# First layer of a graph network: sums and extrema in one bank and one add, two zero matmuls an entry

## The chip, the cores and the metric

One core of one Trainium2 chip. The time is device microseconds of one execution of the whole kernel, median of the runs given. In what follows PE is TensorE, PEld its weight loads, DVE VectorE, ACT ScalarE, POOL GpSimd and SP SyncE.

## What is computed

A graph of 6250 nodes with 128 features and 206250 directed edges, sorted by destination, goes through three message-passing layers (one that aggregates in four ways, a graph convolution, a graph attention) with norms between them. The change touches only the edge loop of the first layer:

```
z2 = concatenate([node_feat[src], node_feat[dst], edge_feat], axis=-1)
e = relu(z2 @ W_pre + b_pre)
s  = segment_sum(e, dst);  sq = segment_sum(e * e, dst)
mx = segment_max(e, dst);  mn = segment_min(e, dst)
deg = segment_sum(1, dst)
```

Mean, deviation, maximum and minimum of each node then go into a two-stage network. The layers after it are the same before and after the change.

## The kernel before

Edges are in chunks of 512, destinations in windows of W = 64 nodes. An entry is one chunk seen through one window; a chunk whose edges span more than 64 nodes gets more entries, and there are 404 of them. `acc` (128 x 5 x 6400, f32, in SBUF) holds per node column the sum, the sum of squares, the count, and the maximum and minimum. The loop does for each entry:

- SP (`loads`, L520 and after, and `load_dst`) fetches the source numbers (`ms`), the edge features (`ZR`, partitions 0 to 63), 64 rows of the destination table (`WB`), the destination numbers broadcast over 64 partitions (`dstb`), and the destinations of last edges (`md`). POOL (`gather`) gathers 512 source rows (`G`) in four indirect DMAs, one for 128 rows. ACT's queue loads the segment masks (`mm2`).
- DVE: `d1` makes the one-hot of destinations in partitions 64 to 127 of `ZR`; `d2` adds the product `Z` and the gathered rows into `EE`; `hot` makes the one-hot `oh` by edges (0 to 3 for the sums, 4 to 7 for the last edge of each node); `d3` runs a maximum scan and a minimum scan over the transposed edges `ET` into `ST`; `d4a` adds sums and count from PSUM (`TT`) into `acc`, `d4b` the extrema.
- ACT: `a1` relu and square, in `EE`; `half` casts half of `oh` to bf16 (`ohb`); `a2a`, `a2b` copy the transposed scans from PSUM (`BK`) to `BS`; `e1`, `e2` copy the two products out of PSUM to `SN1` and `SN2`.
- PE: `p1` is `Z` = `ZR`^T `WB`; `p2` transposes `EE` into `ET` and makes the sums, `oh`^T times `EE`, into `S1`, in two halves of 64 columns; `t1` counts (four bf16 matmuls with ones) and turns `SN1` into `TT`; `t2` turns `SN2` into `TT`; `p3a`, `p3b` transpose the maximum and minimum scan back, one after the other through the one bank `BK`; `p4` is `oh`^T times `BS` into `S2`. `warm` is a matmul of zeros, 512 columns of bf16, into the bank that is written next; it stands ahead of `p1`, of `p2` and of `p3a`.

The order on each engine is written out by hand, by `pipeline`: a list of (lag, step), and in turn i the step runs for entry i - lag. The loop is unrolled four times. In PE's list p3a, t2, t1, p1, p3b, p2, p4 the sums of entry i - 3 and `p4` of entry i - 5 are neighbours at the end of a turn. In DVE's list `d2` comes first, for entry i - 2, and waits for the sums of entry i - 4. The waits are by semaphores with counts; what a step waits for can be read at its head. All eight banks of PSUM are in use: `Z` and `ET` two each, `S1`, `S2`, `BK`, `TT`.

Of the kernel before, what the change touches and what calls it, by code (L numbers as in the profile page):

```python
# [6 lines left out]
BF16 = mybir.dt.bfloat16  # L7
# [435 lines left out]
def phase_l0(nc, d, v):  # L443
# [10 lines left out]
    with ExitStack() as ph:  # L454
# [4 lines left out]
        dstb = sbt(ph, "dstb", [128, 4, CH])  # L459
        mm2 = sbt(ph, "mm2", [128, 4, 2, CH], BF16)  # L460
        G = sbt(ph, "G", [128, 4, 4, 128])
        EE = sbt(ph, "EE", [128, 2, 2, CH])
        oh = sbt(ph, "oh", [128, 4, 8, W])
        ohb = sbt(ph, "ohb", [128, 2, 4, W], BF16)
        ST = sbt(ph, "ST", [128, 2, 2, CH])
        BS = sbt(ph, "BS", [128, 2, 2, CH])
        SN1 = sbt(ph, "SN1", [128, 128])
        zw = sbt(ph, "zw0", [128, 128], BF16)
        zm = sbt(ph, "zm0", [128, CH], BF16)
        SN2 = sbt(ph, "SN2", [128, 128])  # L470
        Z = [pst(ph, f"Z{k}", [128, CH]) for k in range(2)]
        ET = [pst(ph, f"ET{k}", [128, CH]) for k in range(2)]
        S1 = pst(ph, "S1", [128, 512])
        S2 = pst(ph, "S2", [128, 512])
        BK = pst(ph, "BK", [128, CH])
        TT = pst(ph, "TT", [128, 512])
        S1v = TT[:, 0:3 * W].rearrange("p (a n) -> p a n", a=3)
        S2v = TT[:, 4 * W:6 * W].rearrange("p (a n) -> p a n", a=2)
# [12 lines left out]
        s_a1 = sem("l_a1")  # L491
        s_p2 = sem("l_p2")
        s_p2t = sem("l_p2t")
        s_e1 = sem("l_e1")
        s_t1 = sem("l_t1")
# [5 lines left out]
        s_e2 = sem("l_e2")  # L501
        s_t2 = sem("l_t2")
        s_d4a = sem("l_d4a")
        s_d4b = sem("l_d4b")
# [8 lines left out]
        def _(e):  # L513
# [6 lines left out]
            def loads(j):  # L520
# [5 lines left out]
                gathered, done = 64 * j.uses(4, -1), j.at(-3)  # L526
# [3 lines left out]
                if not j.first(4):  # L530
                    wait_sync(e, s_p1, done, s_sync)
                e.dma_start(ZR[0:64, k, :], src[1]).then_inc(l_in[k], 16)
                e.dma_start(WB[64:128, k, :], src[2]).then_inc(l_in[k], 16)
                if not j.first(4):
                    wait_sync(e, s_zr, done, s_sync)
                e.dma_start(dstb[64:128, k, :], src[3]).then_inc(l_db[k], 16)
# [28 lines left out]
        def _(e):  # L565
            e.memset(zw[:, :], 0.0).then_inc(s_i, 1)
            e.memset(zm[:, :], 0.0).then_inc(s_i, 1)
            e.memset(ST[:, :, :, :], 0.0).then_inc(s_i, 1)
            e.wait_ge(s_i, 3)
            T = load_T(e, tb, 0)  # L570

            def d1(j):
                k = j.slot(4)
                wait(e, l_db[k], 16 * j.uses(4))
                if not j.first(4):
                    wait(e, s_p1, j.at(-3))
                e.tensor_scalar(ZR[64:128, k, :], dstb[64:128, k, :], baseF[64:128, ds(j.at(), 1)], nid[64:128, 0:1],  # L577
                                ALU.subtract, ALU.is_equal).then_inc(s_zr, 1)

            def d2(j):  # L580
                wait(e, s_p1, j.at(1))
                wait(e, l_g[j.slot(4)], 64 * j.uses(4))
                if not j.first(2):
                    wait(e, s_p2, j.at(-1))
                e.tensor_tensor(EE[:, j.slot(2), 1, :], Z[j.slot(2)][:, :],
                                G[:, j.slot(4), :, :].rearrange("p s f -> p (s f)"), ALU.add).then_inc(s_d2, 1)

            def hot(j):
                k = j.slot(4)
                wait(e, l_md[k], 16 * j.uses(4))  # L590
                if not j.first(4):
                    wait(e, s_p4, j.at(-3))
# [1660 lines left out]
```

## Time and profile before

| | us |
|---|---|
| median of 3 runs | 5772.62 |
| lowest, highest | 5770.69, 5776.23 |
| the profiled execution | 5773.65 |
| its span, first to last instruction | 5771.7 |

The profiled execution's core had a mean granted clock of 0.947. The first layer's edge loop runs from about 130 us to 2276 us of the span; the preparation of tables lies ahead of it, the other two layers behind. In the profile a group is one line of the kernel on one engine; `idle before` is the time in which the engine did nothing just before the group's instructions, with what ended it. "issue" means that nothing the profile shows ended it.

### The profile page before, as it was taken

What the parts mean: (1) busy time and instruction counts of PE and PEld (TensorE: products, weight loads), DVE (VectorE), ACT (ScalarE), POOL (GpSimd) and SP (SyncE); (2) the same over time, 40 slices, a digit from 0 to 9 for tenths busy, and PEclk for the clock granted to TensorE, in tenths of its full rate; (3) what the DMA queues carried; (4) which work ended last, traced back from release to release, by engine and by line L of the source; (5) the groups of instructions that cost most, each with busy time, mean ns of one, the idle gap of its engine ahead of it and who ended that gap; (6) DMA issues with size and microseconds to landing.
All of it is one profiled execution on the core that took longest, in us unless ns stands there. A gap on an engine that the chain in (4) does not pass through costs nothing. (4 is left out here: it accounts for less than half of the span.)

```text
span 5771.7 us, 176467 instructions
## 1 busy us (share of the span) xinstructions
PE 5106.0 (88%) x41872; PEld 4051.2 (70%) x42482; DVE 4775.1 (83%) x12693; ACT 2880.1 (50%) x6715; POOL 3884.4 (67%) x3976
## 2 busy tenths in 40 slices
PE   3999999999999997968888866999999999999993
PEld 3888888888888886447777754666666666666663
DVE  4999999999999997767777756888888888888887
ACT  1565666656665654123333334555555555555556
POOL 2777777777777774047777724777777777777772
PEclk7999999999999998969888877999999999999996
DMA  6666666666666664322222212222222222222221
GB/s 156 160 159 159 157 158 156 159 156 158 157 157 157 158 157 119 99 53 54 54 54 53 54 33 43 54 53 53 54 53 53 53 53 53 53 53 53 53 53 48
DMA packets 667245, 544.72 MB, mean 94 GB/s; under 512 B 365794, under 2 KB 544171, under 8 KB 666853
## 3 DMA queue, kind: packets, MB, share of 16 engines
q0 software_dynamic: 126336, 262.13, 19.1%
q1 hardware_dynamic: 415050, 163.69, 12.4%
q10 hardware_dynamic: 125724, 117.57, 7.8%
q14 instruction: 108, 0.88, 0.1%
q8 instruction: 27, 0.44, 0.0%
HBM read 517.22 MB, written 25.61 MB: 94 GB/s over the span
## 5 line engine op out<-in xcount | busy, mean ns | idle before, releaser
L1766 POOL DMA_INDIRECT Gt<-TAB,metat x1632 | 1597.2, 979 | 646.9 <-issue 496.4
L559 POOL DMA_INDIRECT G<-Atab,ms x1616 | 1575.6, 975 | 576.9 <-issue 460.3
L1256 POOL DMA_INDIRECT Gc<-XS,metac x672 | 645.3, 960 | 241.8 <-issue 189.0
L1806 DVE SCALAR_TENSOR_TENSOR M<-neqt,Gt 128x256 f32<-128x256 f32 x816 | 311.0, 422 | 309.0 <-DMA Gt<-TAB,metat 308.8
L663 ACT COPY BS<-BK 128x512 f32<-128x512 f32 x808 | 465.6, 576 | 198.9 <-PE BK L752 191.1
L1401 ACT COPY acc<-CP 128x300 f32<-128x300 f32 x630 | 269.5, 428 | 555.1 <-PE CP L1439 552.4
L606 DVE TENSOR_TENSOR_SCAN ST<-mm,ST,ET 128x512 f32<-128x512 bf16 x404 | 516.7, 1279 | 0.1
L608 DVE TENSOR_TENSOR_SCAN ST<-mm,ST,ET 128x512 f32<-128x512 bf16 x404 | 506.9, 1255 | 0.0
L702 PE MATMUL Z<-WB,ZR 128*128 128x128 f32 x3232 | 429.3, 276 | 66.8 <-DVE ZR L577 66.6
L752 PE MATMUL BK<-ident,ST 128*128 128x128 f32 x3232 | 485.1, 273 | 2.4 <-ACT BS L663 1.8
L1970 PE MATMUL SR<-P,Gt 128*128 128x128 f32 x3264 | 473.7, 288 | 0.0
L1970 PEld LDWEIGHTS SR<-P,Gt 128*128 128x128 f32 x3264 | 395.8, 191 | 70.2 <-issue 70.2
L720 PE MATMUL S<-EE,oh 128*64 128x128 f32 x6464 | 442.5, 279 | 0.0
L702 PEld LDWEIGHTS Z<-WB,ZR 128*128 128x128 f32 x3232 | 428.5, 193 | 12.0
L1414 PE MATMUL OT<-acc 128*128 128x180 f32 x2100 | 431.7, 332 | 0.5 <-ACT acc L1401 0.5
L1904 ACT ACTIVATE EX<-TE,nl 128x512 f32<-128x512 f32 x408 | 294.7, 722 | 270.9 <-ACT nl L1897 140.2
L639 ACT ACTIVATE EE<-EE 128x512 f32<-128x512 f32 x404 | 255.1, 631 | 346.3 <-issue 273.1
L769 PE MATMUL S<-BS,oh 128*64 128x128 f32 x6464 | 422.5, 273 | 1.4 <-issue 1.4
L752 PEld LDWEIGHTS BK<-ident,ST 128*128 128x128 f32 x3232 | 392.6, 141 | 32.7 <-issue 2.5
L1327 DVE TENSOR_SCALAR O<-iotaD,VA 128x300 bf16<-128x300 f16 x1260 | 400.3, 322 | 1.0
L720 PEld LDWEIGHTS S<-EE,oh 128*64 128x64 f32 x6464 | 345.0, 137 | 67.7 <-issue 67.7
L1439 PE MATMUL CP<-O 128*128 128x300 bf16 x1260 | 301.2, 326 | 78.3 <-DVE O L1327 74.8
(291 smaller groups left out, 11448.5 us busy)
## 6 DMA issues: line engine op xcount, KB each, us to landing
mm<-MM ACTq DMA_DIRECT2D x404, 256.0 KB
ZR<-in_eft SPq DMA_DIRECT2D x404, 128.0 KB
dstb<-DF SPq DMA_DIRECT2D x404, 128.0 KB
Gt<-TAB,metat POOLq DMA_INDIRECT x1632
G<-Atab,ms POOLq DMA_INDIRECT x1616
ad<-ADT SPq DMA_DIRECT2D x816, 0.2 KB
WB<-Btab SPq DMA_DIRECT2D x404, 32.0 KB
Gc<-XS,metac POOLq DMA_INDIRECT x672
```

What stands on the lines that cost most here:

```text
L559: e.indirect_dma_start(G[:, k, s, :], None, Atab, bass.IndirectOffsetOnAxis(ap=ms[:, k, s:s + 1], axis=0)).then_inc(l_g[k], 16)
L606: e.tensor_tensor_scan(ST[:, q, 0, :], mm2[:, k, 0, :], ET[q][:, :], ST[:, 1 - q, 0, CH - 1:CH], ALU.mult, ALU.max)
L608: e.tensor_tensor_scan(ST[:, q, 1, :], mm2[:, k, 1, :], ET[q][:, :], ST[:, 1 - q, 1, CH - 1:CH], ALU.max, ALU.min).then_inc(s_d3, 1)
L663: e.copy(BS[:, q, a, :], BK[:, :]).then_inc(s_a2[a], 1)
L702: mm = e.matmul(Z[q][:, s * 128:(s + 1) * 128], ZR[:, k, s * 128:(s + 1) * 128], WB[:, k, :], start=True, stop=True)
L720: mm = e.matmul(S1[a * 64:(a + 1) * 64, 0:128], oh[:, k, s, :], EE[:, q, a, s * 128:(s + 1) * 128], start=(s == 0), stop=(s == 3))
L752: mm = e.transpose(BK[:, s * 128:(s + 1) * 128], ST[:, q, a, s * 128:(s + 1) * 128], ident[:, :])
L769: mm = e.matmul(S2[a * 64:(a + 1) * 64, 0:128], oh[:, k, 4 + s, :], BS[:, q, a, s * 128:(s + 1) * 128], start=(s == 0), stop=(s == 3))
L1256: e.indirect_dma_start(G[:, k, s, :], None, XS, bass.IndirectOffsetOnAxis(ap=meta[:, k, s:s + 1], axis=0)).then_inc(l_g[k], 16)
L1414: mm = e.matmul(OT[k][:, 0:DB], acc[:, 0, h * 128:(h + 1) * 128], C[k][:, h, :], start=(h == 0), stop=(h == NB - 1))
L1766: e.indirect_dma_start(G[:, k, s, :], None, TAB, bass.IndirectOffsetOnAxis(ap=meta[:, k, s:s + 1], axis=0)).then_inc(l_g[k], 16)
L1970: m = e.matmul(SR[q][:, 0:2 * W], G[:, k, s, 0:128], P[:, q, s * 128:(s + 1) * 128], start=(s == 0), stop=(s == 3))
```

## The change

- `S1` and `S2` become one bank `S`, sums in columns 0 to 127, extrema in 128 to 255. `SN1`, `SN2` become `SN` (256 columns), with one copy (`sums` on ACT) instead of two.
- `t1` and `t2` become one step `across` at lag 6: counts, then both turns. One add `d4` of 5 x 64 columns at lag 7 takes the place of `d4a` and `d4b`.
- The bank that is freed goes to `BK`: one for each scan. `p3a` and `p3b` stand one after the other at the head of PE's turn, without `warm`.
- The sums are a step of their own, `sums` at lag 5 instead of 3, between `p1` and `p2`. `EE` and `ohb` get four slots for two.
- `dstb` goes: the destination numbers are loaded into partitions 64 to 127 of `ZR`, and `d1` works in place; the load now waits for `p1` instead of for the mask.
- The zero matmul's moving operand is `zw` broadcast; `zm` goes. Orders on DVE and ACT change as the lists show.

```diff
--- before.py
+++ after.py
@@ -456,26 +456,20 @@
         md = sbt(ph, "md", [128, 4, 8], I32)
         ZR = sbt(ph, "ZR", [128, 4, CH])
         WB = sbt(ph, "WB", [128, 4, 128])
-        dstb = sbt(ph, "dstb", [128, 4, CH])
         mm2 = sbt(ph, "mm2", [128, 4, 2, CH], BF16)
         G = sbt(ph, "G", [128, 4, 4, 128])
-        EE = sbt(ph, "EE", [128, 2, 2, CH])
+        EE = sbt(ph, "EE", [128, 4, 2, CH])
         oh = sbt(ph, "oh", [128, 4, 8, W])
-        ohb = sbt(ph, "ohb", [128, 2, 4, W], BF16)
+        ohb = sbt(ph, "ohb", [128, 4, 4, W], BF16)
         ST = sbt(ph, "ST", [128, 2, 2, CH])
         BS = sbt(ph, "BS", [128, 2, 2, CH])
-        SN1 = sbt(ph, "SN1", [128, 128])
+        SN = sbt(ph, "SN", [128, 256])
         zw = sbt(ph, "zw0", [128, 128], BF16)
-        zm = sbt(ph, "zm0", [128, CH], BF16)
-        SN2 = sbt(ph, "SN2", [128, 128])
         Z = [pst(ph, f"Z{k}", [128, CH]) for k in range(2)]
         ET = [pst(ph, f"ET{k}", [128, CH]) for k in range(2)]
-        S1 = pst(ph, "S1", [128, 512])
-        S2 = pst(ph, "S2", [128, 512])
-        BK = pst(ph, "BK", [128, CH])
+        S = pst(ph, "S", [128, 512])
+        BK = [pst(ph, f"BK{a}", [128, CH]) for a in range(2)]
         TT = pst(ph, "TT", [128, 512])
-        S1v = TT[:, 0:3 * W].rearrange("p (a n) -> p a n", a=3)
-        S2v = TT[:, 4 * W:6 * W].rearrange("p (a n) -> p a n", a=2)
         l_we = sem("l_we")
         l_ms = [sem(f"l_ms{k}") for k in range(4)]
         l_md = [sem(f"l_md{k}") for k in range(4)]
...
@@ -523,17 +514,15 @@
                 e0 = c * CH
                 src = (d["meta"][ds(c, 1), :, 0:4].rearrange("a p s -> (a p) s"), d["eft"][:, ds(e0, CH)],
                        Btab[ds(b, 64), :], DF[ds(e0, CH)].partition_broadcast(64))
-                gathered, done = 64 * j.uses(4, -1), j.at(-3)
+                gathered = 64 * j.uses(4, -1)
                 if not j.first(4):
                     wait_sync(e, l_g[k], gathered, s_sync)
                 e.dma_start(ms[:, k, :], src[0]).then_inc(l_ms[k], 16)
                 if not j.first(4):
-                    wait_sync(e, s_p1, done, s_sync)
+                    wait_sync(e, s_p1, j.at(-3), s_sync)
+                e.dma_start(ZR[64:128, k, :], src[3]).then_inc(l_db[k], 16)
                 e.dma_start(ZR[0:64, k, :], src[1]).then_inc(l_in[k], 16)
                 e.dma_start(WB[64:128, k, :], src[2]).then_inc(l_in[k], 16)
-                if not j.first(4):
-                    wait_sync(e, s_zr, done, s_sync)
-                e.dma_start(dstb[64:128, k, :], src[3]).then_inc(l_db[k], 16)
 
             def load_dst(j):
                 k = j.slot(4)
@@ -564,25 +553,22 @@
         @blk.vector
         def _(e):
             e.memset(zw[:, :], 0.0).then_inc(s_i, 1)
-            e.memset(zm[:, :], 0.0).then_inc(s_i, 1)
             e.memset(ST[:, :, :, :], 0.0).then_inc(s_i, 1)
-            e.wait_ge(s_i, 3)
+            e.wait_ge(s_i, 2)
             T = load_T(e, tb, 0)
 
             def d1(j):
                 k = j.slot(4)
                 wait(e, l_db[k], 16 * j.uses(4))
-                if not j.first(4):
-                    wait(e, s_p1, j.at(-3))
-                e.tensor_scalar(ZR[64:128, k, :], dstb[64:128, k, :], baseF[64:128, ds(j.at(), 1)], nid[64:128, 0:1],
+                e.tensor_scalar(ZR[64:128, k, :], ZR[64:128, k, :], baseF[64:128, ds(j.at(), 1)], nid[64:128, 0:1],
                                 ALU.subtract, ALU.is_equal).then_inc(s_zr, 1)
 
             def d2(j):
                 wait(e, s_p1, j.at(1))
                 wait(e, l_g[j.slot(4)], 64 * j.uses(4))
-                if not j.first(2):
-                    wait(e, s_p2, j.at(-1))
-                e.tensor_tensor(EE[:, j.slot(2), 1, :], Z[j.slot(2)][:, :],
+                if not j.first(4):
+                    wait(e, s_p2, j.at(-3))
+                e.tensor_tensor(EE[:, j.slot(4), 1, :], Z[j.slot(2)][:, :],
                                 G[:, j.slot(4), :, :].rearrange("p s f -> p (s f)"), ALU.add).then_inc(s_d2, 1)
 
             def hot(j):
@@ -590,6 +576,7 @@
                 wait(e, l_md[k], 16 * j.uses(4))
                 if not j.first(4):
                     wait(e, s_p4, j.at(-3))
+                    wait(e, s_a1, j.at(-3))
                 e.scalar_tensor_tensor(oh[:, k, :, :], iotaW[:, :].unsqueeze(1).to_broadcast([128, 8, W]),
                                        baseF[:, ds(j.at(), 1)],
                                        md[:, k, :].unsqueeze(2).to_broadcast([128, 8, W]),
@@ -613,38 +600,32 @@
             def base(j):
                 keep(e, regs, j, base_of(e, tb, j))
 
-            def d4(j, S, n, lo, s_in, s_out):
+            def d4(j):
                 b = kept(e, regs, j)
-                wait(e, s_in, j.at(1))
+                wait(e, s_t, j.at(1))
                 if not j.first(1):
-                    wait(e, s_out, j.at())
-                a = acc[:, lo:lo + n, ds(b, W)]
-                e.tensor_tensor(a, a, S, ALU.add).then_inc(s_out, 1)
-
-            def d4a(j):
-                d4(j, S1v, 3, 0, s_t1, s_d4a)
-
-            def d4b(j):
-                d4(j, S2v, 2, 3, s_t2, s_d4b)
-
-            pipeline(e, T, U, D, [(4, base), (2, d2), (0, d1), (2, hot), (4, d4a), (6, d4b), (4, d3)])
+                    wait(e, s_d4, j.at())
+                a = acc[:, 0:5, ds(b, W)]
+                e.tensor_tensor(a, a, TT[:, 0:5 * W].rearrange("p (a n) -> p a n", a=5), ALU.add).then_inc(s_d4, 1)
+
+            pipeline(e, T, U, D, [(4, base), (0, d1), (7, d4), (2, d2), (2, hot), (4, d3)])
 
         @blk.scalar
         def _(e):
             T = load_T(e, tb, 0)
 
             def a1(j):
-                q = j.slot(2)
+                q = j.slot(4)
                 wait(e, s_d2, j.at(1))
                 e.activation(EE[:, q, 0, :], EE[:, q, 1, :], ACT.Relu).then_inc(s_r, 1)
                 wait(e, s_r, j.at(1))
                 e.activation(EE[:, q, 1, :], EE[:, q, 0, :], ACT.Square).then_inc(s_sq, 1)
 
             def half(j):
-                q = j.slot(2)
+                q = j.slot(4)
                 wait(e, s_oh, j.at(1))
-                if not j.first(2):
-                    wait(e, s_t1, j.at(-1))
+                if not j.first(4):
+                    wait(e, s_t, j.at(-3))
                 e.copy(ohb[:, q, :, :], oh[:, j.slot(4), 0:4, :]).then_inc(s_a1, 1)
 
             def masks(j):
@@ -660,7 +641,7 @@
                 wait(e, s_p3[a], j.at(1))
                 if not j.first(2):
                     wait(e, s_p4, j.at(-1))
-                e.copy(BS[:, q, a, :], BK[:, :]).then_inc(s_a2[a], 1)
+                e.copy(BS[:, q, a, :], BK[a][:, :]).then_inc(s_a2[a], 1)
 
             def a2a(j):
                 back(j, 0)
@@ -668,28 +649,22 @@
             def a2b(j):
                 back(j, 1)
 
-            def e1(j):
-                wait(e, s_p2, j.at(1))
-                if not j.first(1):
-                    wait(e, s_t1, j.at())
-                e.copy(SN1[:, :], S1[:, 0:128]).then_inc(s_e1, 1)
-
-            def e2(j):
+            def sums(j):
                 wait(e, s_p4, j.at(1))
                 if not j.first(1):
-                    wait(e, s_t2, j.at())
-                e.copy(SN2[:, :], S2[:, 0:128]).then_inc(s_e2, 1)
-
-            pipeline(e, T, U, D, [(5, a2a), (1, masks), (2, a1), (5, a2b), (2, half), (3, e1), (5, e2)])
+                    wait(e, s_t, j.at())
+                e.copy(SN[:, :], S[:, 0:256]).then_inc(s_e, 1)
+
+            pipeline(e, T, U, D, [(5, a2a), (5, a2b), (2, a1), (1, masks), (3, half), (5, sums)])
 
         @blk.tensor
         def _(e):
             e.wait_ge(l_we, 64)
-            e.wait_ge(s_i, 3)
+            e.wait_ge(s_i, 2)
             T = load_T(e, tb, 0)
 
             def warm(bank):
-                e.matmul(bank[:, :], zw[:, :], zm[:, :], start=True, stop=True)
+                e.matmul(bank[:, :], zw[:, :], zw[:, :].unsqueeze(1).to_broadcast([128, 4, 128]), start=True, stop=True)
 
             def p1(j):
                 q, k = j.slot(2), j.slot(4)
@@ -704,52 +679,32 @@
                 mm.then_inc(s_p1, 1)
 
             def p2(j):
-                q, k = j.slot(2), j.slot(4)
+                q = j.slot(2)
                 wait(e, s_sq, j.at(1))
                 if not j.first(2):
                     wait(e, s_d3, j.at(-1))
                 warm(ET[q])
                 for s in range(4):
-                    mm = e.transpose(ET[q][:, s * 128:(s + 1) * 128], EE[:, q, 0, s * 128:(s + 1) * 128], ident[:, :])
+                    mm = e.transpose(ET[q][:, s * 128:(s + 1) * 128], EE[:, j.slot(4), 0, s * 128:(s + 1) * 128], ident[:, :])
                 mm.then_inc(s_p2t, 1)
-                wait(e, s_oh, j.at(1))
+
+            def across(j):
+                wait(e, s_a1, j.at(1))
+                wait(e, s_e, j.at(1))
                 if not j.first(1):
-                    wait(e, s_e1, j.at())
+                    wait(e, s_d4, j.at())
                 for s in range(4):
-                    for a in range(2):
-                        mm = e.matmul(S1[a * 64:(a + 1) * 64, 0:128], oh[:, k, s, :], EE[:, q, a, s * 128:(s + 1) * 128],
-                                      start=(s == 0), stop=(s == 3))
-                mm.then_inc(s_p2, 1)
-
-            def t1(j):
-                q = j.slot(2)
-                wait(e, s_a1, j.at(1))
-                wait(e, s_e1, j.at(1))
-                wait(e, s_d4b, j.at(-2))
-                if not j.first(1):
-                    wait(e, s_d4a, j.at())
-                for s in range(4):
-                    e.matmul(TT[:, 2 * W:3 * W], onesb[:, :], ohb[:, q, s, :], start=(s == 0), stop=(s == 3))
-                e.transpose(TT[:, 0:128], SN1[:, :], ident[:, :]).then_inc(s_t1, 1)
-
-            def t2(j):
-                wait(e, s_e2, j.at(1))
-                wait(e, s_d4a, j.at(min(2, -j.o)))
-                if not j.first(1):
-                    wait(e, s_d4b, j.at())
-                e.transpose(TT[:, 4 * W:6 * W], SN2[:, :], ident[:, :]).then_inc(s_t2, 1)
+                    e.matmul(TT[:, 2 * W:3 * W], onesb[:, :], ohb[:, j.slot(4), s, :], start=(s == 0), stop=(s == 3))
+                e.transpose(TT[:, 0:2 * W], SN[:, 0:128], ident[:, :])
+                e.transpose(TT[:, 3 * W:5 * W], SN[:, 128:256], ident[:, :]).then_inc(s_t, 1)
 
             def p3(j, a):
                 q = j.slot(2)
                 wait(e, s_d3, j.at(1))
-                if a == 1:
-                    wait(e, s_a2[0], j.at(1))
-                elif not j.first(1):
-                    wait(e, s_a2[1], j.at())
-                if a == 0:
-                    warm(BK)
+                if not j.first(1):
+                    wait(e, s_a2[a], j.at())
                 for s in range(4):
-                    mm = e.transpose(BK[:, s * 128:(s + 1) * 128], ST[:, q, a, s * 128:(s + 1) * 128], ident[:, :])
+                    mm = e.transpose(BK[a][:, s * 128:(s + 1) * 128], ST[:, q, a, s * 128:(s + 1) * 128], ident[:, :])
                 mm.then_inc(s_p3[a], 1)
 
             def p3a(j):
@@ -757,20 +712,29 @@
 
             def p3b(j):
                 p3(j, 1)
+
+            def sums(j):
+                k = j.slot(4)
+                wait(e, s_oh, j.at(1))
+                if not j.first(1):
+                    wait(e, s_e, j.at())
+                for s in range(4):
+                    for a in range(2):
+                        mm = e.matmul(S[a * 64:(a + 1) * 64, 0:128], oh[:, k, s, :], EE[:, k, a, s * 128:(s + 1) * 128],
+                                      start=(s == 0), stop=(s == 3))
+                mm.then_inc(s_p2, 1)
 
             def p4(j):
                 q, k = j.slot(2), j.slot(4)
                 for a in range(2):
                     wait(e, s_a2[a], j.at(1))
-                if not j.first(1):
-                    wait(e, s_e2, j.at())
                 for s in range(4):
                     for a in range(2):
-                        mm = e.matmul(S2[a * 64:(a + 1) * 64, 0:128], oh[:, k, 4 + s, :], BS[:, q, a, s * 128:(s + 1) * 128],
+                        mm = e.matmul(S[a * 64:(a + 1) * 64, 128:256], oh[:, k, 4 + s, :], BS[:, q, a, s * 128:(s + 1) * 128],
                                       start=(s == 0), stop=(s == 3))
                 mm.then_inc(s_p4, 1)
 
-            pipeline(e, T, U, D, [(5, p3a), (6, t2), (4, t1), (1, p1), (5, p3b), (3, p2), (5, p4)])
+            pipeline(e, T, U, D, [(5, p3a), (5, p3b), (1, p1), (5, sums), (3, p2), (6, across), (5, p4)])
 
     recycle(nc, used)
 
```

## Rows read from the trace of the kernel before

**Rows 1.** The page: busy time by engine, and the granted clock in 40 slices.

```profile
PE 5106.0 (88%) x41872; PEld 4051.2 (70%) x42482; DVE 4775.1 (83%) x12693; ACT 2880.1 (50%) x6715; POOL 3884.4 (67%) x3976
...
PEclk7999999999999998969888877999999999999996
```

**Rows 2.** Busy us by engine (instructions), clock, DMA share, GB/s, 700 to 1100.

```profile
700.00:1100.00 400.00, 395.98 (x4573) 355.65 (x4649) 378.71 (x534) 240.85 (x534) 296.32 (x305) 1.00 0.61 157
```

**Rows 3.** Groups: line, engine, op, shapes, count; busy, mean; idle before; 300 to 2200.

```profile
L752 PEld LDWEIGHTS BK<-ident,ST 128*128 128x128 f32 x2896 | 352.0, 141 | 27.0
...
L720 PEld LDWEIGHTS S<-EE,oh 128*64 128x64 f32 x5792 | 308.8, 136 | 60.5 <-issue 60.5
...
L639 ACT ACTIVATE EE<-EE 128x512 f32<-128x512 f32 x362 | 228.6, 631 | 247.3 <-issue 247.3
...
L692 PEld LDWEIGHTS BK<-zm,zw 128*128 128x128 bf16 x362 | 34.6, 96 | 62.0 <-issue 62.0
```

**Rows 4.** Timeline of PE over one turn: start, us, line, tiles, shape, count.

```profile
1006.93 0.39 PE L692 MATMUL BK<-zm,zw 128*128 128x512 bf16 x1
1007.16 0.60 PE L752 MATMUL BK<-ident,ST 128*128 128x128 f32 x4
1007.59 0.27 PE L740 MATMUL TT<-ident,SN 128*128 128x128 f32 x1
1007.70 0.28 PE L732 MATMUL TT<-ohb,onesb 128*128 128x64 bf16 x4
1007.82 0.31 PE L733 MATMUL TT<-ident,SN 128*128 128x128 f32 x1
1007.96 0.38 PE L692 MATMUL Z<-zm,zw 128*128 128x512 bf16 x1
1008.18 1.05 PE L702 MATMUL Z<-WB,ZR 128*128 128x128 f32 x8
1009.07 0.60 PE L752 MATMUL BK<-ident,ST 128*128 128x128 f32 x4
1009.72 0.60 PE L713 MATMUL ET<-ident,EE 128*128 128x128 f32 x4
1010.25 1.09 PE L720 MATMUL S<-EE,oh 128*64 128x128 f32 x16
1011.17 1.04 PE L769 MATMUL S<-BS,oh 128*64 128x128 f32 x16
1012.15 0.39 PE L692 MATMUL BK<-zm,zw 128*128 128x512 bf16 x1
```

**Rows 5.** Timeline of DVE over the same turn.

```profile
1006.24 0.69 DVE L585 TENSOR_TENSOR EE<-Z,G 128x512 f32<-128x512 f32 x1 [0.26 <-PE S L720]
...
1008.37 0.57 DVE L622 TENSOR_TENSOR acc<-acc,TT 128x192 f32 x2
1008.86 1.28 DVE L606 TENSOR_TENSOR_SCAN ST<-mm,ST,ET 128x512 f32<-128x512 bf16 x1
1010.05 1.25 DVE L608 TENSOR_TENSOR_SCAN ST<-mm,ST,ET 128x512 f32<-128x512 bf16 x1
1011.39 0.69 DVE L585 TENSOR_TENSOR EE<-Z,G 128x512 f32<-128x512 f32 x1
```

**Rows 6.** The two adds into acc, groups kept apart by shape, 300 to 2200.

```profile
L622 DVE TENSOR_TENSOR acc<-acc,TT 128x192 f32 x362 | 128.3, 354 | 23.2 <-PE TT L733 17.8 <-issue 0.2
...
L622 DVE TENSOR_TENSOR acc<-acc,TT 128x128 f32 x362 | 104.2, 288 | 0.0
```

**Rows 7.** POOL's gathers from 151.8 to 542.2 us: the group, first gather, first after.

```profile
L559 POOL DMA_INDIRECT G<-Atab,ms x304 | 297.8, 979 | 92.6 <-issue 83.2 <-DMA ms<-in_meta 6.7 <-DVE EE L585 2.7
...
151.82 0.94 POOL L559 DMA_INDIRECT G<-Atab,ms  x1 [0.30 <-issue]
...
542.23 0.94 POOL L559 DMA_INDIRECT G<-Atab,ms  x1 [0.30 <-issue]
```

**Rows 8.** The waits of SyncE's queue: total us, times, longest; 300 to 2200.

```profile
SPq L428 <- PE Z L702: 88.0, 247, 0.6
```

More of the change, by code:

```diff
@@ L491, in phase_l0 @@
         s_a1 = sem("l_a1")
+        s_p2t = sem("l_p2t")
         s_p2 = sem("l_p2")
-        s_p2t = sem("l_p2t")
-        s_e1 = sem("l_e1")
-        s_t1 = sem("l_t1")
+        s_e = sem("l_e")
+        s_t = sem("l_t")
         s_d3 = sem("l_d3")
@@ L500, in phase_l0 @@
         s_p4 = sem("l_p4")
[L501 to L504, printed above, removed]
+        s_d4 = sem("l_d4")
         s_i = sem("l_i")
```

## The prediction

> **What bounds the kernel now.** I read the page first, for the engines' shares over the span: TensorE (PE) leads, and its granted clock is full in the slices of the first layer after its start [rows 1]. The change lies in the first layer's loop alone, so next comes the table by stretches: between 700 and 1100 us PE is busy 395.98 of 400 us, VectorE (DVE) 378.71, GpSimd (POOL) 296.32, ScalarE (ACT) 240.85, at clock 1.00 [rows 2]. A busy PE is not proof by itself, since the ends of matmuls are modelled. The groups of 300 to 2200 us give the period, 1900 us for 362 zero matmuls of `BK`, one an entry, so 5.25 us an entry, and show who waits: PE's weight loads sit idle only before the zero matmul of `BK` and before the sums (62.0 and 60.5 us over 362 entries, 0.17 us each), and nothing that PE waits for is named there [rows 3]. The timeline of PE over one turn of its order shows the same from near: starts follow one another from 1006.93 to the same zero matmul at 1012.15, 5.22 us, every group starting before the one ahead has ended or as it ends [rows 4]. The period of 5.25 holds a further 0.03, a share of the turn of the loop, once in four entries. So PE's own throughput sets the period.
>
> DVE is close behind. In its timeline one turn is from 1006.24 to 1011.39; its one idle stretch, 0.26 us, waits for the sums of two entries back (EE's slot) [rows 5]. POOL is closer than its busy share says: each gather takes 0.98 us and is followed by 0.30 us of idle time that nothing ends. How fast it could go is seen where it isn't held back, early on, when it is behind and catches up: 304 gathers, 76 entries, between 151.82 and 542.23 us, so 390.41 / 76 = 5.137 us an entry [rows 7]. That is the floor under any speed-up of the others.
>
> **The change, part by part, on PE.** The terms are distances between starts in one turn, since durations overlap.
> - The zero matmul ahead of `BK` goes: 1006.93 to 1007.16, -0.23 us [rows 4].
> - The four count matmuls and the two turns of the sums stay, six matmuls of the same shapes, at another place (1007.59 to 1007.96, 0.37 us together) [rows 4]. 0.
> - The two scan transposes become neighbours. Each is 0.43 us for four (1007.16 to 1007.59) wherever it stands [rows 4]. The wait of the second for ACT's copy of the first goes; it was never late (no idle time before L752), so 0.
> - The sums leave their place beside the extrema's product (`p4`). In before, the two groups with 64-column weights (L720, L769) are neighbours, so an entry has one passage from full-width to half-width weights and one back. After, the order is full (p3a, p3b, p1), half (sums), full (p2, across), half (p4): two of each. The prices in rows: into half width, L713 to L720 is 0.53 for four transposes against 0.43 for the same four of `BK` without a passage, +0.10; back, L769 to L692 is 0.98 against 0.92 for L720 to L769, which are the same sixteen records without a passage, +0.06 [rows 4]. Together +0.16.
> - The passage back ahead of `p3a` has no zero matmul behind it any more. What that cover was worth no row shows alone. Its bounds: 0, and the difference between the weight loads of an f32 transpose and of the zero matmul, 141 - 96 = 45 ns [rows 3]. I take the middle, +0.02.
>
> Sum on PE: -0.23 + 0.10 + 0.06 + 0.02 = -0.05 us an entry, so 5.20 for 5.25. With 404 entries, -20 us.
>
> The Trainium skill (TensorEngine Tiling, Key Properties) says that a change of tiling mode drains TensorE. This is the rule that speaks against the change; the trace agrees that a passage costs something, 0.10 and 0.06 us by starts, though it can't show that a drain is the reason. The page gives no figure; without the rule the sum would be -0.23 an entry.
>
> **On DVE.** Two adds, 288 and 354 ns long, become one of 320 columns [rows 6]. By the slope, 66 ns for 64 columns, the one takes 354 + 2 x 66 = 486 ns; the two together held DVE for 0.49 from 1008.37 to the scan at 1008.86 [rows 5], since part of them overlaps. So between 0 and 642 - 486 = 156 ns goes from DVE's turn. That is off the path. The mask made in place is the same instruction with the same 64x512 operands; it loses its wait for `s_p1`, which moves to the load. 0. The wait of the sum `d2` for the sums matmuls falls from one entry back to three (EE has four slots), so DVE's idle 0.26 at this place goes. In its stead the add `d4` stands there and waits for `across`, the last group but one of PE's turn. Queued behind it on DVE are d2, hot and the two scans, and PE's next turn waits for the second scan. Counting from the end of `across`, 0.98 before PE's next turn (the length of p4, 1011.17 to 1012.15 [rows 4]): the add takes up to 0.49, and what follows at most what lay from d2 to the end of the scans less the adds, 1011.30 - 1006.24 - 0.49 = 4.57 [rows 5] (less still, as the mask now runs ahead of the add); so the scans end at latest 0.49 + 4.57 - 0.98 = 4.1 us after PE's turn begins, and the next turn, which wants them, begins at 5.2. Slack 1.1 us, enough. `hot` gets a wait for ACT's cast of four entries back, which is long done.
>
> **On ACT.** Busy 240.85 / 76 = 3.2 us an entry, and some 0.68 in issuing the mask's load (247.3 / 362, the idle time before the relu, which the profile puts down to nothing) [rows 2, 3]. Two copies of 128 columns become one of 256. It waits for p4 at the end of PE's turn, and the next turn's first `BS` copy, queued behind it, can't begin before its transposes have ended, 0.60 us into the turn [rows 4]; so the copy is hidden. The masks' DMA now goes behind the relu and square instead of ahead: it is wanted three turns later. 0.
>
> **On the queues.** SyncE issues the same five loads, with one wait fewer; the row of dst numbers now waits for p1 of four entries back instead of for the mask, and moves ahead of two loads. SyncE's waits for p1 are 88.0 us in 247 cases, so it already stands there [rows 8]. The load is used three entries later, some 13 us. 0. POOL's waits, for `s_d2` four entries back, keep their lag.
>
> The start memset that goes and the drain of the pipeline (the add comes one turn later) I take together at 0, within 2 us either way. The profiled execution took 5773.65 us, 1.95 over its span of 5771.70; less 20 it is 5753, and by the median of the three runs, 1 us lower, **5752 us**.
>
> **The rivals.**
> - *POOL takes over* (20 in 100). If the passages cost nothing more, because the 0.10 and 0.06 belong to what stands there and not to the width, PE would need 5.25 - 0.23 = 5.02, under POOL's 5.137. Then the gathers set the pace: (5.25 - 5.137) x 404 = 46 us, so 5727. For it: records of matmuls end by a model, so such small distances may mean something else. Against: the two idle stretches of the weight loads stand at just these two passages [rows 3].
> - *Nothing to be seen* (16 in 100). The pair of passages and the lost cover come to about 0.23, what the zero matmul gave: within 11 us of 5773. For it: my +0.10 and +0.06 are single differences.
> - *The passages cost more than the zero matmul gave* (12 in 100), the case on the slower side. Place: PE before `sums` and before `p4`. Price: the whole idle time of the weight loads, 0.17 for each of the two new ones, +0.34 - 0.23 = +0.11 an entry, 5817. It decides from 0.23 for the pair. Against it: in rows 4 the starts lose less than the loads' idle time, since matmuls run meanwhile.
> - *The granted clock falls* (2 in 100) once a zero matmul is missing between transposes. At full clock in [rows 2]; for a tenth of the layer at half clock PE would need another 200 us. Nothing in the trace leads there: PE has no idle time.
> - *The change doesn't do what it says*, for instance the wait for `across` holds DVE and through it PE: by the slack of 1.1 us no, and it is in the 12 above.
>
> **How the numbers follow.** The forecast (a net -0.02 to -0.09 an entry, 5736 to 5764) has 50 in 100. A measurement of this kernel can tell about 0.2%, 11.5 us, from no change. Faster by more: the forecast but for its edge, 44, and POOL's case, 20: 0.64. Within: 5 of the forecast's edge and 17 of the second rival and of what surrounds it: 0.22. Slower by more: 0.14. The range for 8 in 10 takes in POOL's case to 5724 and, on the other side, the smaller half of the slower case, to 5788.
>
> **What would show it.** In the profile after: no zero matmul with `BK`, 404 fewer of them; weight loads idle by about 0.17 in four places an entry, not two (or the first rival is right); starts of ET's transposes to the counts about 0.43, counts and turns to p4 about 0.1 longer than 0.37; PE without a named wait; DVE idle only before the 128x320 add; the first gather's wait still on DVE and not DVE's on gathers (if DVE waits for `G`, POOL is the bound). The prediction is wrong if 1900 us hold fewer than 362 entries or more than 370, or if a wait of PE for DVE or ACT appears.

## The result: 0.5% slower, and the profile after

The changed kernel took 5796.67 us (median of 5, 5791.65 to 5810.35) beside 5772.62 before, a ratio of 1.0046 (1.0035 to 1.0056). Beside two of the variants on a later chip it was 5792.6 against 5765.23, 1.0043 (1.0027 to 1.006). I had forecast 5752, with 5724 to 5788 for 8 in 10.

On three of the five chips of the experiments (the slow chips below) every kernel was over a third slower, the kernel before 7923 to 8025 us at mean granted clocks of 0.84 to 0.85, with waits of up to several us that the profile puts down to nothing on the core; runs there are held against each other only by ratio, and the same kernels were run again elsewhere.

The page of the changed kernel, its lines on the span, on PE, on the granted clock and on the instruction queue:

```profile
span 5806.8 us, 172535 instructions
...
PE 5185.2 (89%) x42078; PEld 4040.7 (70%) x42078; DVE 4692.2 (81%) x12288; ACT 2787.3 (48%) x6311; POOL 3972.2 (68%) x3976
...
PEclk7999999999999999968899977999999999999996
...
q14 instruction: 361, 2.96, 0.2%
```

The first layer's loop runs at clock 1.00 as before. This profiled execution is 14 us above its kernel's median; the second one of the same kernel (5795.0 us of span) has the same period in the loop, so I read periods here and times from the medians.

The table by stretches, 700 to 1100 us (PE, PEld, DVE, ACT, POOL busy with instructions, clock, DMA share, GB/s), to be read against [rows 2]:

```profile
700.00:1100.00 400.00, 400.00 (x4525) 343.30 (x4526) 357.08 (x454) 226.62 (x452) 307.98 (x302) 1.00 0.63 156
```

PE is busy all the time and DVE only 357 of 400 us: the distance between the two has grown. The groups of 300 to 2200 us, against [rows 3, 6 and 7]:

```profile
L548 POOL DMA_INDIRECT G<-Atab,ms x1433 | 1464.1, 1022 | 437.0 <-issue 345.5 <-DVE EE L571 70.4 <-DMA ms<-in_meta 21.0
...
L707 PEld LDWEIGHTS BK<-ident,ST 128*128 128x128 f32 x2864 | 306.7, 141 | 61.3 <-issue 61.3
...
L723 PEld LDWEIGHTS S<-EE,oh 128*64 128x64 f32 x5734 | 305.7, 136 | 43.1
L733 PEld LDWEIGHTS S<-BS,oh 128*64 128x64 f32 x5728 | 305.3, 136 | 59.9 <-issue 59.9
...
L609 DVE TENSOR_TENSOR acc<-acc,TT 128x320 f32 x358 | 174.9, 488 | 190.6 <-PE TT L699 190.3 <-issue 0.3
...
L667 PEld LDWEIGHTS ET<-zw 128*128 128x128 bf16 x358 | 34.4, 96 | 61.3 <-ACT EE L622 61.3
```

358 entries in 1900 us, 5.307 us an entry for 5.249: 0.058 x 404 = 23 us of the 24 measured. The weight loads are idle 0.17 us in front of `BK`, of `p4` and of the zero matmul of `ET` (the name of ACT beside it is only the semaphore that came last: the same 0.17 stands, without a name, at the passages of the variants). Ahead of `sums` it is 0.12 (43.1 / 358), without a name. A *passage* is a change between full-width groups and the two groups with 64-column weights (`sums`, `p4`), in or out. So there are four such places for two. 358 entries are under the 362 that I had named as the sign of being wrong. The one add takes 488 ns, for 486 forecast, and DVE waits 0.53 us for `across`, as meant. Now the turn of PE, the row that answers to each of [rows 4]:

```profile
1003.38 1.09 PE L707 MATMUL BK<-ident,ST 128*128 128x128 f32 x8
1004.31 0.38 PE L667 MATMUL Z<-zw 128*128 128x512 bf16 x1
1004.53 1.05 PE L677 MATMUL Z<-WB,ZR 128*128 128x128 f32 x8
1005.51 1.09 PE L723 MATMUL S<-EE,oh 128*64 128x128 f32 x16
1006.54 0.39 PE L667 MATMUL ET<-zw 128*128 128x512 bf16 x1
1006.77 0.60 PE L688 MATMUL ET<-ident,EE 128*128 128x128 f32 x4
1007.20 0.28 PE L697 MATMUL TT<-ohb,onesb 128*128 128x64 bf16 x4
1007.32 0.31 PE L698 MATMUL TT<-ident,SN 128*128 128x128 f32 x1
1007.46 0.27 PE L699 MATMUL TT<-ident,SN 128*128 128x128 f32 x1
1007.67 1.09 PE L733 MATMUL S<-BS,oh 128*64 128x128 f32 x16
1008.69 0.77 PE L707 MATMUL BK<-ident,ST 128*128 128x128 f32 x5
```

Starts from 1003.38 to 1008.69, 5.31 us. The two scan transposes together are 0.93 (1003.38 to 1004.31), p1 to `sums` 0.98, `sums` to the zero matmul of ET 1.03, counts and turns to `p4` 0.47, `p4` to the next BK 1.02. In [rows 4] the same groups had 0.43 for each scan (0.86), 0.89, 0.92, 0.37 and 0.98. Only ET's transposes are shorter, 0.43 for 0.53, since no passage follows them any more.

### The profile page after: what moved, and what is told of

The parts are those of the page before. It is cut to its first block and busy times, and to the rows that moved or that the text cites. A ratio compares the mean times of both kernels' runs of the same rounds, so it can differ in the third digit from the quotient of the medians.

```text
span 5806.8 us, 172535 instructions
## 1 busy us (share of the span) xinstructions
PE 5185.2 (89%) x42078; PEld 4040.7 (70%) x42078; DVE 4692.2 (81%) x12288; ACT 2787.3 (48%) x6311; POOL 3972.2 (68%) x3976
## 5 line engine op out<-in xcount | busy, mean ns | idle before, releaser
L548 POOL DMA_INDIRECT G<-Atab,ms x1616 | 1650.3, 1021 | 532.6 <-issue 394.6
L644 ACT COPY BS<-BK 128x512 f32<-128x512 f32 x808 | 434.2, 589 | 84.8 <-PE BK L707 66.7
L1876 ACT COPY P<-PT 128x512 f32<-128x512 f32 x408 | 238.7, 585 | 446.4 <-PE PT L1920 423.0
L707 PE MATMUL BK<-ident,ST 128*128 128x128 f32 x3232 | 442.6, 280 | 5.1 <-DVE ST L595 5.1
L733 PE MATMUL S<-BS,oh 128*64 128x128 f32 x6464 | 442.1, 279 | 0.0
L656 ACT COPY SN<-S 128x256 f32<-128x256 f32 x404 | 150.5, 373 | 557.9 <-PE S L733 526.3
L707 PEld LDWEIGHTS BK<-ident,ST 128*128 128x128 f32 x3232 | 346.9, 141 | 74.5 <-issue 69.0
L733 PEld LDWEIGHTS S<-BS,oh 128*64 128x64 f32 x6464 | 344.5, 136 | 67.6 <-issue 67.6
L1290 DVE TENSOR_SCALAR O<-iotaD,VA 128x128 bf16<-128x128 f16 x1260 | 324.2, 257 | 67.9 <-issue 31.2
```

The source lines that it names most:

```text
L548: e.indirect_dma_start(G[:, k, s, :], None, Atab, bass.IndirectOffsetOnAxis(ap=ms[:, k, s:s + 1], axis=0)).then_inc(l_g[k], 16)
L644: e.copy(BS[:, q, a, :], BK[a][:, :]).then_inc(s_a2[a], 1)
L707: mm = e.transpose(BK[a][:, s * 128:(s + 1) * 128], ST[:, q, a, s * 128:(s + 1) * 128], ident[:, :])
L733: mm = e.matmul(S[a * 64:(a + 1) * 64, 128:256], oh[:, k, 4 + s, :], BS[:, q, a, s * 128:(s + 1) * 128], start=(s == 0), stop=(s == 3))
```

## Experiments

Three theories. *1, passages*: the second pair of passages between full-width and half-width weights costs more than the zero matmul gave. *2, lost cover*: the missing zero matmul lays weight loads bare. *3, new waits*: of the one bank `S`, or of the add behind `across`. The kernel before was run beside each variant.

**sums_beside_p4**: the changed kernel, with the sums directly ahead of p4.

```diff
-[(5, p3a), (5, p3b), (1, p1), (5, sums), (3, p2), (6, across), (5, p4)]
+[(5, p3a), (5, p3b), (1, p1), (3, p2), (6, across), (5, sums), (5, p4)]
```

> The changed kernel with one thing moved: in PE's list the sums step stands directly ahead of p4, so an entry has one passage into half-width weights and one back instead of two. Theory 1 (passages): the pair of passages costs about 0.27 us an entry, which I read from the distances between starts in the profile after (sums 1.03, p4 1.02, p1 to sums 0.98, against 0.86 for sixteen or eight records without passages). PE would need 5.307 - 0.27 = 5.04 us, below the 5.137 of the gathers' catching-up rate, so POOL sets the pace: (5.307 - 5.137) x 404 = 69 us less, about 5728. Theory 2 (lost cover: the missing zero matmul exposes weight loads ahead of p3a): the move changes nothing of it, about 5797. Theory 3 (the new waits, of the one bank S or of the add behind across): unchanged or slower, 5797 or more, with a named wait of PE.

On a slow chip: 7751.81 us, 0.9769 of before (0.9748 to 0.979).

> The run sums_beside_p4 once more, as the kernel before took 7947 us beside the first one (5773 in the case's own runs), with waits of many us for signals that the profile can't place: that chip's times can't be held against the terms, which are tenths of a microsecond an entry. Same expectations: theory 1 (passages) 5728; theories 2 (lost cover) and 3 (new waits) 5797 or more.

On another slow chip 7880.19, 0.9837 (0.9801 to 0.9872). And the changed kernel and this one together on a chip with 5765.23 for before:

> The changed kernel itself, so that the variants have it beside them on one chip. On a chip where the kernel before takes 5773 us: 5797. On the kind of chip of the last seven runs (kernel before 7947 to 8025), theory 1: slower than sums_beside_p4 by what across_between is slower than it, 2.1 per cent; theories 2 and 3: as fast as sums_beside_p4.

> The changed kernel with the sums directly ahead of p4, beside the changed kernel on one chip. Theory 1: 5728 where the kernel before takes 5773; else 0.98 of after_c. Theories 2 and 3: as after_c.

5792.6 and **5689.39** us; the variant is 0.9871 of before (0.9854 to 0.9887). One step moved in one list gives 103 us, 0.255 us an entry. Theories 2 and 3 have no place for that. PE's timeline of sums_beside_p4_c over one turn:

```profile
1000.07 1.09 PE L707 MATMUL BK<-ident,ST 128*128 128x128 f32 x8
1001.00 0.38 PE L667 MATMUL Z<-zw 128*128 128x512 bf16 x1
1001.21 1.05 PE L677 MATMUL Z<-WB,ZR 128*128 128x128 f32 x8
1002.10 0.38 PE L667 MATMUL ET<-zw 128*128 128x512 bf16 x1
...
1003.01 0.27 PE L699 MATMUL TT<-ident,SN 128*128 128x128 f32 x1
1003.22 1.09 PE L723 MATMUL S<-EE,oh 128*64 128x128 f32 x16
1004.14 1.04 PE L733 MATMUL S<-BS,oh 128*64 128x128 f32 x16
1005.11 1.09 PE L707 MATMUL BK<-ident,ST 128*128 128x128 f32 x8
```

5.04 from 1000.07 to 1005.11. The scans are 0.93 as in the changed kernel. p1 to the next group is 0.89 for 0.98, `sums` to p4 0.92 for 1.03, p4 to BK 0.97 for 1.02: the 0.25 lies on the three sides where a passage went. The means over the turns of 700 to 1900 us agree with all these distances within 0.01. And it ran faster than theory 1 said (5728), under the floor of 5.137 that I had put under POOL; of that below. Its groups of 300 to 2100 us on POOL and the two idle weight loads, 0.17 each, one pair:

```profile
L548 POOL DMA_INDIRECT G<-Atab,ms x1427 | 1365.6, 957 | 434.8 <-issue 391.6 <-DMA ms<-in_meta 39.0 <-DVE EE L571 4.3
...
L723 PEld LDWEIGHTS S<-EE,oh 128*64 128x64 f32 x5712 | 304.5, 136 | 59.7 <-issue 59.7
...
L707 PEld LDWEIGHTS BK<-ident,ST 128*128 128x128 f32 x2848 | 304.4, 141 | 61.0 <-issue 61.0
```

**across_between**: as above, but `across` (full width) between the sums and p4, so two pairs again.

```diff
+[(5, p3a), (5, p3b), (1, p1), (3, p2), (5, sums), (6, across), (5, p4)]
```

> As sums_beside_p4, but with across (full-width counts and turns) between the sums and p4: two pairs of passages again, and the order of all else as in sums_beside_p4. Theory 1: back at 5797 within 8 us, and slower than sums_beside_p4 by the pair, up to 69 us. Theories 2 and 3: no difference between the two orders beyond 10 us.

7912.51 on the first slow chip, 0.997 of before (0.995 to 0.9989) and 1.021 of sums_beside_p4 there.

> The run across_between once more, for the same reason. Theory 1: 5797 within 8 us, slower than sums_beside_p4_b by up to 69 us. Theories 2 and 3: the two orders within 10 us of each other.

On the second 8045.41, 1.0036 of before (1.0014 to 1.0059), and again 1.021 of sums_beside_p4 (7880.19).

> The changed kernel with sums moved behind ET's transposes but across between sums and p4, on a chip where the kernel before takes about 5770: sums_beside_p4_c (5689 there, the changed kernel 5793) has the same kernel but for across. Theory 1 (two pairs of passages): 5793 within 8 us, a turn of PE of 5.31. If instead the place of the sums in the turn (or its waits for EE and S) made the difference: 5689 within 8 us, a turn of 5.05.

That chip, the third, was slow too (7894.17, 0.9957 of before).

> As for across_between_d, whose chip was again one on which the kernel before takes 7923 us. Where it takes about 5770: theory 1 (two pairs of passages) 5793 within 8 us, a turn of 5.31; if the place of the sums or its waits made the difference, 5689 within 8 us, a turn of 5.05.

Where before takes 5768.54: **5792.25**, 1.0042 (1.0027 to 1.0056), the time of the changed kernel (5792.6 on a chip with 5765.23). It differs from sums_beside_p4 only in what stands between the two half-width groups. Its timeline:

```profile
1004.04 0.60 PE L688 MATMUL ET<-ident,EE 128*128 128x128 f32 x4
1004.57 1.09 PE L723 MATMUL S<-EE,oh 128*64 128x128 f32 x16
1005.60 0.29 PE L697 MATMUL TT<-ohb,onesb 128*128 128x64 bf16 x4
...
1005.87 0.27 PE L699 MATMUL TT<-ident,SN 128*128 128x128 f32 x1
1006.07 1.09 PE L733 MATMUL S<-BS,oh 128*64 128x128 f32 x16
1007.10 1.09 PE L707 MATMUL BK<-ident,ST 128*128 128x128 f32 x8
```

ET's transposes to the sums 0.53 (passage in), sums 1.03 (1004.57 to 1005.60), `across` to p4 0.20, p4 1.03. The lag of the sums, their place behind ET's transposes and the waits of EE and S are the same in both variants, so they are not what costs. The passages are: boundaries between full-width groups, as from p1 to the zero matmul of ET (0.89), carry no such price.

**before_no_zero**: the kernel before, without its zero matmul ahead of the first scan transpose.

```diff
-                if a == 0:
-                    warm(BK)
```

> The kernel before, without its zero matmul ahead of the first scan transpose, nothing else. Theory 1: PE's turn falls by 0.23 less about 0.05 of uncovered weight load, from 5.25 to 5.07, under POOL's 5.137: 5772.6 - 46 = 5727. Theory 2 (the zero matmul was a cover that cost little): between 5760 and 5780.

On the first slow chip 7929.98, 0.998 (0.9962 to 0.9999).

> The run before_no_zero once more, for the same reason. Theory 1: 5727. Theory 2: 5760 to 5780.

On the second 8011.32, 0.9994 (0.9975 to 1.0013).

> The kernel before without the zero matmul ahead of the first scan transpose. Theory 1: 5727 where the kernel before takes 5773. Theory 2: 5760 to 5780.

Where before takes 5765.23: 5748.99, 0.9971 (0.9959 to 0.9982). 16 us, where theory 1 said 46 and theory 2 5760 to 5780; neither. The timeline of the kernel without it, ACT's copy of the extrema's product, then PE and its loads:

```profile
1007.24 0.27 ACT L681 COPY SN<-S 128x128 f32<-128x128 f32 x1 [0.61 <-PE S L767]
...
1007.12 0.66 PE L750 MATMUL BK<-ident,ST 128*128 128x128 f32 x4
...
1007.63 0.32 PE L740 MATMUL TT<-ident,SN 128*128 128x128 f32 x1
...
1007.93 0.18 PEld L732 LDWEIGHTS TT<-ohb,onesb 128*128 128x128 bf16 x4 [0.16 <-issue]
1007.96 0.28 PE L732 MATMUL TT<-ohb,onesb 128*128 128x64 bf16 x4
```

The copy of `SN2` runs from 1007.24 to 1007.51, and the turn of it (`t2`, L740), which waits for it in the code, follows at 1007.63, 0.51 after the scans' transposes began; the counts come another 0.33 later. That is one turn. As means over the turns of 700 to 1900 us the first distance is 0.50 for 0.44 before, the second 0.22 for 0.13, and the one from the last turn (L733) to the zero matmul of `Z` 0.19 for 0.15. So of the 0.23 saved 0.19 comes back. The first 0.06 is lost cover, as in the changed kernel (next variant); the rest is what the chain p4, ACT's copy, t2 explains: with the zero matmul t2's weight load begins 0.15 after the end of the copy in the mean, without it 0.06. No wait is named there and no run moved the copy alone, so that this chain is the cause is argued from order and timing.

**after_with_zero**: the changed kernel with the zero matmul back ahead of p3a.

```diff
+                if a == 0:
+                    warm(BK[0])
```

> The changed kernel with the zero matmul put back ahead of p3a (into the first BK bank). Theory 1: PE's turn 5.307 + 0.23 - 0.05 = 5.49, so 404 x 0.18 = 73 us more, 5870. Theory 2: the cover comes back, so no more than 20 us over 5797, or under it.

On the first slow chip 7922.04, 0.9966 (0.9948 to 0.9983).

> The changed kernel with the zero matmul put back ahead of p3a, on such a chip. In the kernel before its removal brought 16 us and not 46, because t2 then waits for ACT's copy of SN2 (0.50 for 0.44 and 0.19 for 0.11 in the distances). In the changed kernel nothing waits there, so if the zero matmul has its whole price of 0.23 less 0.07 of cover: (5.31 + 0.16) for 5.31, 65 us more, 5858. If it costs 0.04 net as in the kernel before: 5809.

On the third 7899.62, 0.9967 (0.9944 to 0.999). The changed kernel itself was not run on a slow chip; beside across_between, which has its passages and takes its time, these are 10 and 5 us more. So there the zero matmul seems to cost next to nothing, which I can't explain.

> As for after_with_zero_d: the zero matmul at its price less the cover, 5858; at 0.04 net as in the kernel before, 5809.

Where before takes 5768.54: **5866.07**, 1.0169 (1.0152 to 1.0186), 73 us over the changed kernel of the other chip and 74 over across_between on the same one, 0.18 us an entry. Its removal in the changed kernel is thus worth 0.23 less 0.05 of cover. The cover is seen by itself: the eight scan transposes take 0.87 from start to start with the zero matmul ahead and 0.93 without (means). With `across` an iteration later nothing waits for ACT's copy any more: in the changed kernel it ends at 1003.90 and `across` begins at 1007.20. Theory 2 falls, theory 1's 5870 was met.

**no_zeros**: sums_beside_p4 without its two remaining zero matmuls, to take PE off the bound.

```diff
-                warm(Z[q])
-                warm(ET[q])
```

> sums_beside_p4 without its two remaining zero matmuls, so that PE is no longer the bound: its turn would be 5.05 - 0.22 - 0.22 + 0.14 of cover = 4.75. Theory A, the floor of POOL as predicted, 5.137 at best: as sums_beside_p4, 5689 or more. Theory B, POOL's floor is its gather at its shortest, 4 x (0.94 + 0.30) = 4.97 and DVE's about 4.9: a period of 4.97 to 5.03, so 0.02 to 0.08 x 404 = 8 to 32 us less, 5657 to 5681. Theory C, the granted clock falls below 1.00 in the loop without zero matmuls: slower than 5700.

On the third slow chip 7771.71, 0.9817 (0.9775 to 0.9859).

> As for no_zeros: theory A (POOL's floor 5.137) 5689 or more; theory B (gathers at their shortest) 5657 to 5681; theory C (the granted clock falls) slower than 5700.

Where before takes 5768.54: 5727.05, 0.9929 (0.9911 to 0.9946): slower than sums_beside_p4 (on another chip) by 38 us, 34 by their distances from before, with two matmuls of about 0.22 us less on PE an entry. Theory B's 5657 to 5681 is out. The number fits theory A's "or more" and theory C's, but C's reason fails, as the clock in the loop is 1.00:

```profile
700.00:1100.00 400.00, 364.63 (x4514) 332.41 (x4516) 367.64 (x468) 238.01 (x466) 305.17 (x312) 1.00 0.62 160
```

Its waits, 700 to 1900 us:

```profile
PE BK L705 <- DVE ST L595: 98.8, 139, 2.3
...
DVE EE L571 <- DMA G<-Atab,ms: 79.4, 119, 2.2
```

and its groups, 300 to 2100 us:

```profile
L548 POOL DMA_INDIRECT G<-Atab,ms x1402 | 1373.9, 980 | 427.3 <-issue 412.9 <-DMA ms<-in_meta 14.3
...
L593 DVE TENSOR_TENSOR_SCAN ST<-mm,ST,ET 128x512 f32<-128x512 bf16 x350 | 445.9, 1274 | 0.0
```

DVE waits for gathered rows, which it does in none of the other kernels on chips of this kind, and PE for DVE's scans. 350 entries in 1800 us is 5.143. POOL's gathers follow one another with 0.31 us between them throughout and hardly ever wait for a signal (412.9 of the 427.3 us idle have no name), so with PE out of the way POOL sets the pace, at about the 5.137 of [rows 7]. But that is no floor, as theory A had it, since sums_beside_p4 runs at 5.05 with the same gathers. The gathers' mean lengths differ, 980 ns here, 957 in sums_beside_p4_c, 975 in before, 1022 in the changed kernel, and in after_with_zero_e:

```profile
L548 POOL DMA_INDIRECT G<-Atab,ms x1314 | 1399.5, 1065 | 400.4 <-issue 290.4 <-DVE EE L571 76.8 <-DMA ms<-in_meta 33.2
...
L593 DVE TENSOR_TENSOR_SCAN ST<-mm,ST,ET 128x512 f32<-128x512 bf16 x329 | 419.2, 1274 | 0.0
```

What makes them differ is read from the traces in the last section. sums_beside_p4 beats both kernels and was the best of the study.

## Why the prediction was wrong

- *What bounds the kernel*: right. PE's own throughput did, before and after; no named wait of PE's matmuls turned up, and PE is busy 396 and 400 of 400 us.
- *The zero matmul, -0.23, cover +0.02*: the net is -0.18 (after_with_zero_e), so the cover is 0.05 (0.06 by the starts), at the upper bound I had named (141 - 96 ns) or just over it, and not its middle.
- *The moved turns of the sums, 0*: right by luck. In the kernel before, t2 ran just behind ACT's copy, and the zero matmul hid that chain, so far as before_no_zero shows it; the two parts of the change need each other. With only the zero matmul gone it was 0.04 an entry. I had seen no idle time of PE there and took that for no chain.
- *The second pair of passages, +0.10 and +0.06*: this is the step that failed. The runs show 0.255 for my 0.16 (103 us over 404). The mechanism was right, the term mis-sized by 0.10 us, some 38 us in all; the cover makes up the other 12 us between my -20 and the +30 below. My baseline for "no passage" was the 0.92 from L720 to L769. But L720 had itself just come through a passage in, and the first 0.05 of its 0.92 was the rest of it. The clean distances are in the turns above: p4 with both passages 1.02, with only the one out 0.97; sums with both 1.03, with only the one in 0.92. So out costs 0.11, and in costs 0.05 there and 0.09 in the group ahead (0.98 for 0.89): 0.25 together. My +0.10 was the part of the way in that falls on the group ahead, and it held. The 0.05 on the group behind was missing from the way in, and, sitting in my baseline, was taken off the way out too (0.06 for 0.11). I compared a group with one half of the cost with a group with the other half.
- With the terms as measured, -0.18 + 0.255 = +0.075, times 404 = +30 us against +27 measured on that chip (+24 in the case's own runs). The 0.255 was itself taken from the changed kernel, so the test is the other sum, with the 0.18 from after_with_zero_e alone: sums_beside_p4 should lie -0.18 x 404 = -73 us from before, and lies -76. Within 3 us passages and the zero matmul carry the whole change.
- *The slower rival*, 12 in 100, was the right one, though it put the whole price ahead of `sums` and `p4`, and 0.11 of it lies on the way out. Its point of decision is 0.18 for the pair rather than 0.23, by the cover; its price of 0.34 was too high: 0.255 was paid.
- *POOL's floor of 5.137*: false. It is four gathers of 0.98 with 0.30 between them, and that 0.98 is a mean of gathers of 0.94 and longer ones (last section); sums_beside_p4 ran at 5.05. The price of the first rival and theory 1's 5728 rest on this floor. It did no harm to the forecast, which stayed above it.
- *DVE, ACT, the queues, 0*: nothing in the runs speaks against it. The 320-column add took 488 ns for 486.

The Trainium skill (TensorEngine Tiling, Key Properties) says that a change of tiling mode drains TensorE. The runs put 0.255 us on a pair of such changes here; they don't show what happens inside.

## What to carry to other kernels

Keep matmul groups of one tile width together in PE's order: on a PE-bound loop each extra pair of passages cost 0.255 us here, a little more than a 512-column bf16 matmul (0.23). To price a passage by distances between starts, compare a group with itself in another surrounding, or count both of its sides; its neighbour is no clean baseline. And before taking out filler work, look at which chain on another engine ends just behind it: a filler that hides a chain is nearly free (0.04 us here for 0.18), and taking it out pays only when the chain is moved as well. And a rate read from a stretch in which an engine runs free is not its floor, if another engine holds up its instructions.

## What was not expected of the hardware

- POOL's gathers are held up by two of DVE's instructions. Their mean length was 957 ns at a period of 5.05 us, 980 at 5.14, 1022 at 5.31 and 1065 at 5.48. But it is one gather in four that differs in the changed kernel; the others always take 0.94 to 0.96. The long one of two turns of the changed kernel, with what DVE runs as it begins, and an ordinary one:

```profile
1003.70 0.75 DVE L580 SCALAR_TENSOR_TENSOR oh<-iotaW,baseF,md 128x512 f32<-128x512 f32 x1
...
1003.98 1.29 POOL L548 DMA_INDIRECT G<-Atab,ms  x1 [0.30 <-DVE EE L571]
...
1008.08 0.94 POOL L548 DMA_INDIRECT G<-Atab,ms  x1 [0.30 <-issue]
...
1008.97 0.75 DVE L580 SCALAR_TENSOR_TENSOR oh<-iotaW,baseF,md 128x512 f32<-128x512 f32 x1
...
1009.33 1.21 POOL L548 DMA_INDIRECT G<-Atab,ms  x1 [0.30 <-DVE EE L571]
```

  Both end 0.82 us after the end of `hot` (1004.45 to 1005.27, 1009.72 to 1010.54), wherever in it they began. From 700 to 1900 us this holds without exception in the changed kernel and in four of its variants (after, across_between_e, after_with_zero_e, sums_beside_p4_c, no_zeros_e): each gather over 0.97 us (226 of 905, 227 of 905, 220 of 877, 234 of 952, 155 of 934) began while DVE ran `hot` or `d1`, and ended 0.80 to 0.84 us behind it. Gathers that began during the scans or the adds were not held. So the mean length tells how the gathers fall against DVE's turn: in sums_beside_p4_c one in four meets the end of `d1` (0.997 us), in after_with_zero_e one in four the start of `hot` (1.43). Unheld, four would take 4 x (0.94 + 0.31) = 5.0 us, an estimate from these rows. The kernel before shows the same, and besides some long gathers that begin at the end of `d2`, with `d1` behind it. That DVE holds them is read from these ends; why these two instructions do it and the others don't, no run tested.
- The third layer, whose code the change doesn't touch, was granted a lower clock in the changed kernel. The same stretch, in before and in the changed kernel (after_c):

```profile
4300.00:4700.00 400.00, 363.19 (x2222) 251.34 (x2259) 330.21 (x1092) 214.71 (x545) 305.16 (x312) 1.00 0.27 53
```

```profile
4300.00:4700.00 400.00, 370.57 (x2249) 260.55 (x2288) 334.32 (x1096) 209.37 (x550) 304.94 (x313) 0.96 0.27 54
```

0.96 for 1.00, with POOL at the same pace (305.16 and 304.94 us, x312 and x313). Behind the last add of the first layer (at 2276 and 2297 us) the rest of the span is 3495 and 3498 us. So it cost 3 us at most. The variants of the changed kernel had it too (0.91 as the mean from 2300 to 5600 us against 0.94), the kernel before without its zero matmul not. The page also counts 361 packets of the instruction queue for 108 in the kernel before. What ties these to the first layer's code stays open.
